# Relative-position steps on other images and stores of queries and keys inside the image loop of an attention kernel

## Chip, cores and metric

The kernel runs on one NeuronCore of a Trainium2 chip. The metric is the device time of one execution in microseconds. The core has TensorE (PE, matrix products), VectorE (DVE), ScalarE (ACT), GpSimd (POOL) and SyncE (SP), which here only issues DMAs. Each engine works through its own program in order and waits on semaphores that others raise.

## The reference

Four layers with group norm before each: a GRU scan (l0), attention with relative positions (l1), a mixture of experts (l2), and again attention (l3). The change touches both attention layers, which run the same code. There are 16 images of 14 x 14 tokens, 12 heads of 16 channels:

```python
attn = jnp.einsum('bqd,bkd->bqk', q * scale, k)
rel_h = jnp.einsum('bhwc,hkc->bhwk', qr, Rh)
rel_w = jnp.einsum('bhwc,wkc->bhwk', qr, Rw)
bias = rel_h[..., :, None] + rel_w[..., None, :]
attn = attn + bias.reshape(B * nh, N, N)
attn = jax.nn.softmax(attn, axis=-1)
out = jnp.einsum('bqk,bkd->bqd', attn, v)
```

For each query, `rel_h` gives 14 numbers for the key's row and `rel_w` 14 for its column. The kernel appends them to the query vector, and 28 selecting zeros and ones to the key vector, so that one product gives logits with bias.

## The kernel before

All is in `attention_layer` (L746). Heads are taken in three quads of four. For each quad, `item` computes queries and keys for all images and writes them, as a rounded part and a rest, into a tile in SBUF (`qk_a` or `qk_b`). They go through DRAM, since the main loop wants them in another layout: `store_qk` (L908) stores a quad's half in five DMAs (one of 784 KB, four of 392 KB), `load` (L922) brings a pair of heads back in four quarters of three pieces each.

The relative numbers take 14 steps for a quad, `rel` on each engine: steps 0 to 6 of them are **row steps** (key row) and 7 to 13 **column steps** (key column). In a step, TensorE issues six products (L1118 to L1120) into one PSUM bank, ScalarE copies the rounded part out (L1262), VectorE subtracts for the rest (L1332). The row steps' tile is stored by `store_rel` (L916) as two DMAs of 686 KB, likewise the column steps' tile. For quads 1 and 2 both tiles have one place in SBUF (`rel_tiles`), so ScalarE waits in front of the first column step until the row tile has landed (L1259).

Quad 0's relative steps stand ahead of the main loop. The **main loop** has 96 image steps (6 pairs of heads x 16 images), here counted from 0. Quad 1's 14 relative steps are put into images 0 to 31 and quad 2's into 32 to 63, at the places in `REL_STEPS` (L751); the text calls 32 images a group: images 0 to 31 are the first group, 32 to 63 the second. In step i the engines do, in this order:

- TensorE (L1198): logits by query of image i (L1133, two banks that need the maximum of i-1 taken), the relative step if there is one, the values products of image i-4 (L1171, L1172; they need VectorE's copies of i-5), the logits by key of i-1 (L1147, L1154; the latter adds the maxima).
- ScalarE (L1291): two exponentials of image i-2 (L1300, L1303), sometimes a copy of values (L1285), the relative step.
- VectorE (L1370): the maximum of image i (L1375), at i % 4 of 2 or 3 a subtraction for the values (L1365), two copies of the products of i-4 (L1340, and L1343 into a ring of three slots of sums), the relative step (L1332), at i % 8 = 1 a reciprocal of the sums (L1347).
- GpSimd (L1061): the rest of the exponentials, a subtraction of 98 x 784 (L1065).
- SyncE, `main_step` (L965): loads of the next pair, a store of quad 2's queries and keys if one is due (L972), `store_rel` in the step behind the last row or column step (L974), a load of the residual (L977), stores of sums at even steps, loads of sums and stores of their reciprocals every eight steps.

The load of a pair's first piece waits for its quad's ten stores (L930), the load of the relative piece for the quad's four relative stores (L932). SyncE's queue is one queue: a wait in it holds all that follows.

Of the kernel before, what the change touches and what calls it, by code (L numbers as in the profile page):

```python
# [745 lines left out]
def attention_layer(nc, tag, ins, x_in, y_out, qk_dram, rel_dram, sums_dram, rec_dram, given=None, kept=None, extra=(), taken=None, ahead=None, x_here=None, x_stored=None):  # L746
# [1 line left out]
    IMAGES = PAIRS * B  # L748
    LAG = 4
    REL = 14  # L750
    REL_STEPS = (1, 2, 3, 4, 5, 6, 7, 11, 12, 13, 14, 15, 16, 17)  # L751
    S_BANK, R_BANK, T_BANK, O_BANK = 0, 2, 3, 7
    REL0_BANK, V_BANK = 4, 6
    EARLY_V = 16
# [3 lines left out]
    with Scope(nc, tag) as s:  # L758
# [71 lines left out]
        def qk_of(quad):  # L830
            return (qk_a, qk_b, qk_a)[quad]
# [26 lines left out]

        rel_of_step = {2 * B * quad + at: REL * (quad + 1) + j for quad in range(QUADS - 1) for j, at in enumerate(REL_STEPS)}

# [15 lines left out]
        with nc.Block() as block:  # L876
            @block.sync
            def _(sp):
# [29 lines left out]
                def store_qk(quad, half, terms=range(5)):  # L908
                    sp.wait_ge(item_low, NT * quad + 4 * half + 4)
                    cols = slice(half * N // 2, (half + 1) * N // 2)  # L910
                    for n in terms:
                        rows, term, part = ((slice(0, 128), 0, 0), (slice(0, 64), 1, 1), (slice(64, 128), 1, 0),
                                            (slice(0, 64), 2, 0), (slice(64, 128), 2, 1))[n]
                        sp.dma_start(qk_dram[quad, rows, term, cols].bitcast(f32), qk_of(quad)[rows, part, cols].bitcast(f32)).then_inc(qk_stored[quad], 16)

                def store_rel(quad, which):  # L916
                    sp.wait_ge(rel_low, REL * quad + 7 * which + 7)
                    for part in range(2):
                        sp.dma_start(rel_dram[quad, :, 2 * part + which, :].bitcast(f32),
                                     rel_tile(REL * quad + 7 * which)[64 * part:64 * part + 56, :].bitcast(f32)).then_inc(rel_stored, 16)  # L920

                def load(p, part, piece):  # L922
                    quad, at = divmod(p, 2)
                    cols = slice(part * EACH * T, (part + 1) * EACH * T)
                    if piece == 0:
                        if p == 0:
                            sp.wait_ge(filled, 2)
                        else:
                            sp.wait_ge(t_summed, B * (p - 1) + EACH * (part + 1))
                        sp.wait_ge(qk_stored[quad], 160)  # L930
                    if piece == (0 if p == 0 else 2):
                        sp.wait_ge(rel_stored, 64 * (quad + 1))  # L932
                    if p == 0 and piece == 2:
                        sp.wait_ge(q_padded, 1)
                    qk = qk_dram[quad].rearrange("(a g h r) c n -> a g r c h n", a=2, g=2, h=2)[:, at].rearrange("a r c h n -> a (r c) h n")
                    rel = rel_dram[quad].rearrange("(g h r) c n -> g r c h n", g=2, h=2)[at].rearrange("r c h n -> (r c) h n")
                    dst, row, src = ((q, Q_ROWS, qk[0]), (k, Q_ROWS, qk[1]), (q, REL_ROWS, rel))[piece]
                    rows = src.shape[0]
                    sp.dma_start(dst[row:row + rows, :, cols].bitcast(f32), src[:, :, cols].bitcast(f32)).then_inc(quarter_in[part], 16)

                def store_sums(g):
                    p, b = divmod(g, B)
                    sp.wait_ge(sums_kept, g + 1)
                    slot, col = g // 2 % SLOTS, (b - 1) % (B // 2) * T
                    sp.dma_start(sums_dram[p, b // (B // 2), :, col:col + TB], ring[:, slot, :]).then_inc(sums_free[slot], 16)

                def load_sums(h):
                    for slot in range(SLOTS):
                        sp.wait_ge(sums_free[slot], 16 * ((B // 4 * (h + 1) - slot + SLOTS - 1) // SLOTS))
                    if h:  # L950
                        sp.wait_ge(rec_low, h)
                    sp.dma_start(sums[:, :], sums_dram[h // 2, h % 2].rearrange("h (c n) -> (h c) n", n=32)).then_inc(sums_in, 16)

                def store_reciprocals(h):
                    p, half = divmod(h, 2)
                    sp.wait_ge(rec_low, h + 1)
                    sp.dma_start(rec_dram[half, :, 2 * p:2 * p + 2, :].rearrange("a h (c n) -> (h c) a n", n=32).bitcast(f32),
                                 rec_parts[:, :, :].bitcast(f32)).then_inc(rec_stored, 16)
# [6 lines left out]
                def main_step(i):  # L965
                    p, b = divmod(i, B)
                    part, piece = divmod(b - EACH - 1, EACH)
                    if i < IMAGES and p + 1 < PAIRS and part >= 0 and piece < LOADS:
                        load(p + 1, part, piece)
                    if i < IMAGES and p > 0 and part < 0 and piece < LOADS:  # L970
                        load(p, part + PARTS, piece)
                    if i % 5 == 3 and i < 50:  # L972
                        store_qk(2, i // 25, [i // 5 % 5])
                    if i - 1 in rel_of_step and rel_of_step[i - 1] % 7 == 6:  # L974
                        quad, j = divmod(rel_of_step[i - 1], REL)
                        store_rel(quad, j // 7)
                    n = (i - 2 * B - REL_STEPS[-1] - 2) // 4  # L977
                    if i == 2 * B + REL_STEPS[-1] + 2 + 4 * n and 0 <= n < NT:
                        if n == 0:
                            sp.wait_ge(rel_summed, QUADS * REL)  # L980
                            sp.wait_ge(qk_stored[2], 160)
                        cols = slice(n * TB, (n + 1) * TB)
                        sp.dma_start(xy[:CP, :, cols], x_in[:, :, cols]).then_inc(x_in_again, 16)
                    g = i - LAG - 1
                    if g >= 0 and g % 2 == 1:
                        store_sums(g)
                    if i >= 14 and i % 8 == 6:
                        load_sums((i - 14) // 8)
                    if i >= 21 and i % 8 == 5:
                        store_reciprocals((i - 21) // 8)  # L990
# [7 lines left out]
                for part in range(PARTS):  # L998
                    for piece in range(LOADS):
                        load(0, part, piece)  # L1000
                for half in range(2):
                    store_qk(1, half)
                for i in range(IMAGES + LAG + 1):
                    main_step(i)
                store_reciprocals(2 * PAIRS - 2)
# [1255 lines left out]
def build(nc, ins, out):  # L2261
    scratch = {n: nc.dram_tensor(n, sh, f32r if n in ("qk", "rel", "rec") else f32, kind="Internal").ap() for n, sh in
               (("x1", [CP, CB, N]), ("x2", [C, N]), ("x3", [C, N]), ("qk", [QUADS, 128, 3, N]), ("rel", [QUADS, 56, 4, N]), ("sums", [PAIRS, 2, 2, N // 2]), ("rec", [2, 2, HEADS, N // 2]),
                ("rows", [N, 256]), ("picked", [2 * N + BLOCKS * LANES, C]))}

    def halves(x):
        return x.rearrange("(k p) n -> p k n", k=CB)

    with Scope(nc, "to") as s:
        moments, x_stored = s.sb("moments", [128, 2, B, 2]), s.sem("x_stored")  # L2270
        first = Ahead(nc, "l1")
        x_sb = first.place(AT_Q, CB, N)[:CP]
        averages = [first.place(AT_AVERAGES, CP)[:CP], first.place(AT_AVERAGES + CP, CB, 2, 128)[:CP]]
        ahead = dict(xh=first.place(0, CB, N, dt=f32r), weights=first.weights()[:4], avg=dict(avg=first.place(AT_AVG, CP)[:CP]))
        gru_layer(nc, ins, ins["x"], scratch["x1"], x_sb, x_stored, moments, ahead)
        attention_layer(nc, "l1", ins, scratch["x1"], halves(scratch["x2"]), scratch["qk"], scratch["rel"], scratch["sums"], scratch["rec"],
                        kept=moments, extra=((averages[0], ins["group_avg"]), (averages[1], ins["avg_out128"])), taken=moments[:CP], ahead=ahead, x_here=x_sb, x_stored=x_stored)
        third = Ahead(nc, "l3")
        later = dict(weights=third.weights(), avg=dict(avg=third.place(AT_AVG, 2, 2, 128), avg_out=third.place(AT_AVG + 512, 2, CB, CP)))
        experts_layer(nc, ins, scratch["x2"], scratch["x3"], scratch, moments, later, averages)  # L2280
        attention_layer(nc, "l3", ins, halves(scratch["x3"]), out, scratch["qk"], scratch["rel"], scratch["sums"], scratch["rec"], given=moments, ahead=later)
# [132 lines left out]
```

## Time and profile before

| | us |
|---|---|
| median of 3 runs | 1782.19 (1781.6 to 1787.44) |
| profiled execution | 1781.53 |
| its span on the core | 1779.3 |
| PE / DVE / ACT / POOL busy | 1477.8 / 1251.0 / 899.5 / 800.3 |

The span is the stretch from the first to the last instruction that the profiler shows; 2.2 us of the execution lie around it. Busy time is a sum over stages. The main loop of l1 runs from 643 to about 900 us, that of l3 from 1472 to about 1731 us. L numbers are lines of the kernel before; "SPq" is SyncE's queue.

### The profile page before, as it was taken

The page shows a single profiled execution, that of the slowest core. Times are in us where ns is not written, and L with a number is a line of the kernel's source. Part 1 is how long each engine was busy: PE and PEld are TensorE (multiplying, and loading weights), DVE is VectorE, ACT ScalarE, POOL GpSimd, SP SyncE. Part 2 cuts the span into 40 slices and gives each one's busy share as a digit, 9 for nine tenths or more (in the row PEclk, how much of TensorE's full clock was granted, in tenths as well). Part 3 has the DMA queues.
Part 4 walks back from the last instruction along what each step waited for, and adds up shares of the span by engine and source line. Part 5 has one row for each costly group of instructions (what it writes and reads, how often), then busy time and mean ns, then how long its engine had stood idle before and what let it go on. Part 6 is the DMA issues. An engine that isn't in the chain of part 4 may idle for free. (4 is left out here: it accounts for less than half of the span.)

```text
span 1779.3 us, 50706 instructions
## 1 busy us (share of the span) xinstructions
PE 1477.8 (83%) x19315; PEld 1308.6 (74%) x19315; DVE 1251.0 (70%) x4156; ACT 899.5 (51%) x1894; POOL 800.3 (45%) x888
## 2 busy tenths in 40 slices
PE   4868888888876886989976989899998697888977
PEld 4757777777765685878965667688884587787976
DVE  7877877877878656878856694544446646887874
ACT  3633333333345665767833433555553555666862
POOL 2812222222226054758952210556651415676974
PEclk9955555555558898999987589999995689999998
DMA  3000000000002585658415304333225458666812
GB/s 88 1 21 4 4 4 4 4 4 4 4 4 84 152 241 150 154 138 172 96 37 160 126 14 148 114 96 93 87 78 154 145 149 266 162 140 145 162 31 58
DMA packets 71882, 164.52 MB, mean 92 GB/s; under 512 B 17842, under 2 KB 43066, under 8 KB 69148
## 3 DMA queue, kind: packets, MB, share of 16 engines
q1 hardware_dynamic: 66268, 148.44, 31.6%
q0 software_dynamic: 5376, 12.85, 2.4%
q8 instruction: 156, 2.56, 0.6%
q14 instruction: 82, 0.67, 0.1%
HBM read 93.84 MB, written 67.42 MB: 91 GB/s over the span
## 5 line engine op out<-in xcount | busy, mean ns | idle before, releaser
L1065 POOL TENSOR_TENSOR l_arena<-l_arena,l_arena 98x784 fp32r<-98x784 f32 x192 | 360.5, 1881 | 136.5 <-ACT l_arena L1303 132.0
L514 PE MATMUL gru_ps_r<-gru_hp,gru_wp 128*128 128x16 f16 x3920 | 199.7, 176 | 68.3 <-DVE gru_hp L489 68.3
L514 PEld LDWEIGHTS gru_ps_r<-gru_hp,gru_wp 128*128 128x128 f16 x3920 | 150.4, 105 | 88.7 <-DVE gru_hp L489 88.7
L1300 ACT ACTIVATE l_arena<-l_ps 98x784 fp32r<-98x784 f32 x192 | 158.6, 826 | 103.7 <-PE l_ps L1154 101.7
L1375 DVE TENSOR_REDUCE l_mt<-l_ps 98x4 fp32r<-98x784 f32 x192 | 186.8, 973 | 27.4 <-PE l_ps L1133 22.9
L514 PE MATMUL gru_ps_n<-gru_hp,gru_wp 128*128 128x16 f16 x3920 | 191.2, 174 | 0.0
L567 POOL TENSOR_TENSOR gru_kept<-gru_keep,l0s_state 128x32 f32<-128x32 f32 x196 | 49.3, 252 | 305.9 <-ACT gru_keep L582 305.9
L1171 PE MATMUL l_ps<-l_arena,l_arena 128*66 128x196 f32 x768 | 162.7, 264 | 22.3 <-DVE l_arena L1343 20.7
L580 ACT ACTIVATE gru_reset<-gru_ps_r,gru_unscale 128x32 f32<-128x32 f32 x196 | 56.5, 288 | 216.9 <-PE gru_ps_r L514 216.9
L1172 PE MATMUL l_ps<-l_arena,l_arena 128*66 128x196 f32 x768 | 158.9, 259 | 0.0
L1303 ACT ACTIVATE l_arena<-l_ps 98x784 f32<-98x784 f32 x192 | 157.2, 819 | 0.0
L514 PEld LDWEIGHTS gru_ps_n<-gru_hp,gru_wp 128*128 128x128 f16 x3920 | 150.0, 104 | 0.0
L1171 PEld LDWEIGHTS l_ps<-l_arena,l_arena 128*66 128x66 f32 x768 | 108.9, 142 | 37.8 <-issue 20.1
L1172 PEld LDWEIGHTS l_ps<-l_arena,l_arena 128*66 128x66 f32 x768 | 109.5, 143 | 1.1
L1133 PE MATMUL l_ps<-l_arena,l_arena 128*98 128x196 f32 x768 | 104.0, 258 | 6.7 <-DVE l_mt L1375 4.0
L1154 PE MATMUL l_ps<-l_unit,l_mt 98*98 98x196 f32 x768 | 105.3, 260 | 0.0
L1147 PE MATMUL l_ps<-l_arena,l_arena 128*98 128x196 f32 x768 | 103.9, 259 | 0.0
L1340 DVE COPY l_arena<-l_ps 64x196 f32<-64x196 f32 x192 | 67.6, 352 | 50.1 <-PE l_ps L1172 47.2
L1118 PE MATMUL l_ps<-l_arena,l_arena 128*56 128x224 f32 x168 | 58.9, 351 | 48.7 <-DVE l_arena L1332 45.8
L1262 ACT ACTIVATE l_arena<-l_ps 56x448 fp32r<-56x448 f32 x84 | 63.1, 751 | 68.0 <-PE l_ps L1120 46.5
L2215 DVE TENSOR_TENSOR l_arena<-mx_ps,l_arena 128x512 fp32r<-128x512 f32 x56 | 38.7, 692 | 83.1 <-ACT l_arena L2023 83.1
L1332 DVE TENSOR_TENSOR l_arena<-l_ps,l_arena 56x448 fp32r<-56x448 f32 x84 | 65.0, 775 | 41.0 <-ACT l_arena L1262 39.2
(386 smaller groups left out, 4512.9 us busy)
## 6 DMA issues: line engine op xcount, KB each, us to landing
l_arena<-qk SPq DMA_DIRECT2D x96, 294.0 KB
qk<-l_arena SPq DMA_DIRECT2D x48, 392.0 KB, 6.0
rel<-l_arena SPq DMA_DIRECT2D x24, 686.0 KB
l_arena<-rel SPq DMA_DIRECT2D x48, 343.0 KB
qk<-l_arena SPq DMA_DIRECT2D x12, 784.0 KB, 10.5
l_arena<-in_experts_dram SPq DMA_DIRECT2D x8, 1152.0 KB, 7.5
l_arena<-x SPq DMA_DIRECT2D x24, 294.0 KB, 5.5
l_arena<-x SPq DMA_DIRECT2D x24, 196.0 KB, 4.2
```

The lines of the kernel that those rows point to most:

```text
L514: last = pe.matmul(out[:, b, B * m:B * m + B], wp[:, wi, g, m, :], hp[:, b, part, B * k:B * k + B], start=False, stop=True, skip_group_che ...
L1065: pool.tensor_tensor(pl[g % LOWS][:TH, :, :], p32[:TH, g % 2, :, :], ph[:TH, g % 4, :, :].bitcast(f32), ALU.subtract).then_inc(pl_ready, 1)
L1133: last = pe.matmul(ps[:TH, S_BANK + head, half * T:half * T + T], q[:, head, queries], k[:, head, keys], start=True, stop=True)
L1147: pe.matmul(bank[:, half * T:half * T + T], k[:, head, keys], q[:, head, queries], start=half == 0, stop=False, skip_group_check=True)
L1154: last = pe.matmul(bank[:, :, half * TH:(half + 1) * TH], mt[:TH, g % 2, n:n + 1].to_broadcast([TH, TH]), both, start=False, stop=half == ...
L1171: pe.matmul(out, values, ph[:, g % 4, head, cols], start=head == 0 and keys == 0, stop=False)
L1172: last = pe.matmul(out, values, pl[g % LOWS][:, head, cols], start=False, stop=head == 1 and keys == 1)
L1300: act.activation(ph[:TH, g % 4, :, :], banks, ACT.Exp).then_inc(p_high, 1)
L1303: act.activation(p32[:TH, g % 2, :, :], banks, ACT.Exp).then_inc(p_ready, 1)
L1332: dve.tensor_tensor(rel_out(r, 64), rel_sums(r), rel_out(r, 0).bitcast(f32), ALU.subtract).then_inc(rel_low, 1)
L1340: dve.tensor_copy(o_quad[p // 2][row:row + 64, b * T:(b + 1) * T], ps[:64, O_BANK, :T]).then_inc(o_kept, 1)
L1375: dve.tensor_reduce(mt[:TH, i % 2, :], ps[:TH, S_BANK:S_BANK + 2, :TB].rearrange("p c (h k) -> p c h k", h=2), AXIS.X, ALU.max, negate=Tru ...
```

## The change

```diff
-    REL_STEPS = (1, 2, 3, 4, 5, 6, 7, 11, 12, 13, 14, 15, 16, 17)
+    REL_STEPS = (0, 1, 2, 3, 4, 5, 6, 10, 12, 14, 16, 18, 20, 21)
...
-                    if i % 5 == 3 and i < 50:
-                        store_qk(2, i // 25, [i // 5 % 5])
+                    if 9 <= i < 19:
+                        store_qk(1, (i - 9) // 5, [(i - 9) % 5])
+                    if 23 <= i < 53 and i % 3 == 2:
+                        store_qk(2, (i - 23) // 15, [(i - 23) // 3 % 5])
...
-                for half in range(2):
-                    store_qk(1, half)
                 for i in range(IMAGES + LAG + 1):
                     main_step(i)
```

The row steps move from images 1 to 7 to images 0 to 6 of each group, the column steps from 11 to 17 to 10, 12, 14, 16, 18, 20 and 21. The ten stores of quad 1, all issued ahead of the loop, are issued one a step at steps 9 to 18. Quad 2's ten stores go from steps 3, 8, ..., 48 to 23, 26, ..., 50. What hangs on `REL_STEPS` moves with it: the stores of relative tiles from steps 8 and 18 of a group to 7 and 22, and the residual's eight loads (L977) from 51, 55, ... to 55, 59, .... No instruction is added or removed.

## Rows read from the trace of the kernel before

**Rows 1.** The page's head: the span.

```profile
span 1779.3 us, 50706 instructions
```

**Rows 2.** Windows: us, PE, PEld, DVE, ACT, POOL busy, clock, DMA share, GB/s.

```profile
643.04:738.82 95.78, 76.23 (x685) 70.23 (x686) 68.76 (x118) 60.29 (x88) 59.19 (x38) 0.93 0.72 200
738.82:830.65 91.83, 80.04 (x725) 73.79 (x726) 74.91 (x131) 62.49 (x95) 61.87 (x41) 0.96 0.63 145
830.65:895.83 65.18, 62.31 (x637) 59.30 (x637) 58.22 (x116) 52.40 (x81) 61.56 (x41) 1.00 0.50 100
...
1472.57:1564.31 91.74, 76.05 (x685) 69.73 (x686) 68.43 (x117) 60.31 (x88) 59.08 (x38) 0.96 0.76 211
1564.31:1657.04 92.73, 80.94 (x725) 75.07 (x726) 74.91 (x131) 62.46 (x95) 61.93 (x41) 0.94 0.63 144
```

**Rows 3.** Timeline (start, us, engine, line), ScalarE: the first column step of each group.

```profile
680.62 0.92 ACT L1262 ACTIVATE l_arena<-l_ps 56x448 fp32r<-56x448 f32 x1 [9.18 <-DMA rel<-l_arena]
...
772.59 0.92 ACT L1262 ACTIVATE l_arena<-l_ps 56x448 fp32r<-56x448 f32 x1 [2.12 <-DMA rel<-l_arena]
...
1507.61 0.93 ACT L1262 ACTIVATE l_arena<-l_ps 56x448 fp32r<-56x448 f32 x1 [6.63 <-DMA rel<-l_arena]
...
1598.93 0.93 ACT L1262 ACTIVATE l_arena<-l_ps 56x448 fp32r<-56x448 f32 x1 [2.03 <-DMA rel<-l_arena]
```

**Rows 4.** Timeline, VectorE: last row steps of three groups, and a wait at step 10.

```profile
663.96 0.62 DVE L1332 TENSOR_TENSOR l_arena<-l_ps,l_arena 56x448 fp32r<-56x448 f32 x1
...
763.00 0.62 DVE L1332 TENSOR_TENSOR l_arena<-l_ps,l_arena 56x448 fp32r<-56x448 f32 x1
...
1493.50 0.62 DVE L1332 TENSOR_TENSOR l_arena<-l_ps,l_arena 56x448 fp32r<-56x448 f32 x1
...
1502.02 0.36 DVE L1343 COPY l_arena<-l_ps 2x196 f32<-2x196 f32 x1 [2.62 <-DMA sums<-l_arena]
```

**Rows 5.** Timeline, VectorE: from one column step to the next (steps 15, 16).

```profile
698.29 0.92 DVE L1332 TENSOR_TENSOR l_arena<-l_ps,l_arena 56x448 fp32r<-56x448 f32 x1
699.25 0.98 DVE L1375 TENSOR_REDUCE l_mt<-l_ps 98x4 fp32r<-98x784 f32 x1
701.46 0.35 DVE L1340 COPY l_arena<-l_ps 64x196 f32<-64x196 f32 x1 [1.23 <-PE l_ps L1172]
701.84 0.36 DVE L1343 COPY l_arena<-l_ps 2x196 f32<-2x196 f32 x1
702.23 0.92 DVE L1332 TENSOR_TENSOR l_arena<-l_ps,l_arena 56x448 fp32r<-56x448 f32 x1
```

**Rows 6.** Timeline, TensorE: the same column step.

```profile
699.27 0.39 PE L1118 MATMUL l_ps<-l_arena,l_arena 128*56 128x224 f32 x1 [0.69 <-DVE l_arena L1332]
...
700.51 0.28 PE L1171 MATMUL l_ps<-l_arena,l_arena 128*66 128x196 f32 x1
...
701.25 0.52 PE L1147 MATMUL l_ps<-l_arena,l_arena 128*98 128x196 f32 x4
701.61 0.53 PE L1154 MATMUL l_ps<-l_unit,l_mt 98*98 98x196 f32 x4
```

**Rows 7.** Timeline, VectorE and GpSimd: two pairs of operations that meet.

```profile
691.92 1.76 DVE L1365 TENSOR_TENSOR l_arena<-l_arena,l_arena 98x128 fp32r<-98x128 f32 x1
...
691.67 1.86 POOL L1065 TENSOR_TENSOR l_arena<-l_arena,l_arena 98x784 fp32r<-98x784 f32 x1 [1.50 <-ACT l_arena L1303]
...
758.31 0.28 DVE L1365 TENSOR_TENSOR l_arena<-l_arena,l_arena 98x128 fp32r<-98x128 f32 x1
...
758.35 1.97 POOL L1065 TENSOR_TENSOR l_arena<-l_arena,l_arena 98x784 fp32r<-98x784 f32 x1 [1.23 <-ACT l_arena L1303]
```

**Rows 8.** TensorE at step 19: timeline, then a window (columns of Rows 2).

```profile
710.58 0.40 PE L1171 MATMUL l_ps<-l_arena,l_arena 128*66 128x196 f32 x1 [1.58 <-DVE l_arena L1343]
...
711.00:713.00 2.00, 2.00 (x14) 2.00 (x14) 1.34 (x4) 0.00 (x0) 0.96 (x3) 0.50 0.84 257
```

**Rows 9.** The stores at L914 issued from 636 to 650 us: time to landing.

```profile
DMA to landing us min/median/max: 13.7/16.1/24.7
```

## The prediction

> **What bounds the kernel now.** I read the profile page first for the span [rows 1], then the windows of the main loop of both attention layers [rows 2]. There, 32 images ("a group") without relative steps take 65.18 us, 2.04 us an image, and TensorE is busy for 62.31 of them. A group that carries 14 relative steps takes 91.83 us (layer l1, second group), and TensorE is busy for 80.04 only. The first groups carry the same work and take 95.78 and 91.74 us. So each group with relative steps costs 27 to 31 us more than a plain one, and TensorE's own part in that is about half. The rest is waits, and the change moves just the steps that cause them. Two kinds stand out.
>
> First, the column tile takes the place of the row tile in SBUF (`rel_tiles`), so ScalarE may write the first column step only when the row tile has landed in DRAM (L1260). It waited 9.18 us for that in l1's first group and 6.63 in l3's, but 2.12 and 2.03 in the second groups [rows 3]. From the end of VectorE's last row step to ScalarE's first column step are 16.0 and 13.5 us in first groups, and 9.0 in a second one [rows 3, 4]. The transfer is the same. What differs is the queue: in first groups the ten stores of quad 1's queries and keys stand ahead of it, and they took 13.7 to 24.7 us from issue to landing [rows 9].
>
> Second, a chain through three engines in consecutive column steps. VectorE's rows show it from one step to the next [rows 5]: the step's subtraction (0.92 us, L1332), the maximum (0.97, L1375), 1.23 us idle until TensorE's values product is done, two copies (0.38 each with their pitch), the next subtraction. That is 3.94 us, from 698.29 to 702.23. TensorE starts its relative products 0.06 us after the subtraction ends, issues them for 1.24 us, and only then the values products, 0.74 us [rows 6], because its program has the relative step in front of them. So in this stretch an image lasts 3.93 us instead of 2.04, and neither engine is full.
>
> **The change part by part.**
>
> *Column wait.* The stores of quad 1 leave the place ahead of the loop and go out one a step at steps 9 to 18. The row store goes out at SyncE's step 7 (before: 8), the first column step is step 10 (before: 11), so three plain images lie between, as before. Ahead of it in the queue is then what a second group has: three loads. So I give the first groups the second groups' wait. By ScalarE's idle time that is 9.18 - 2.12 = 7.1 us in l1. In l3 it is 6.63 - 2.12 = 4.5, with VectorE's wait of 2.62 us for a slot of the sums [rows 4] in the shadow of the same column wait, and not added. Sum: -11.6 us. The second groups keep their 2.1 us, as their row store still has its 9 us to go. Bounds: -15 if the queue is even emptier (each group's wait halved), 0 if the first groups still wait as long.
>
> *Columns apart.* Laid out in program order, a column step and the plain image behind it give this loop: logits by query 0.37 (four products of that size lie 0.36 apart, [rows 6]), relative products 1.24, values products 0.74 and 0.21 until VectorE sees them, two copies 0.77, subtraction 0.95, the maximum of the next image 1.03, after which TensorE may overwrite the logits bank for the image after next. That is 5.31 us for the pair. Before, one consecutive column step and one plain image elsewhere took 3.93 + 2.04 = 5.97. Each column step that gets a plain neighbour saves 0.66 us. Before, one of the seven had one (step 17); after, six do, as only 20 and 21 adjoin. Five times 0.66 is 3.3 us a group, and -13.2 us for four groups. TensorE's own issue time in the pair is 2 x 1.84 + 1.24 = 4.9, so it cannot go below 5 us for a pair; the lower bound is -20.
>
> *What takes most of that back.* VectorE's subtraction for the values (L1365), twice in four images, shows a duration of 0.28 us when it starts just before GpSimd's subtraction, and 1.76 when it starts 0.25 us into one: it ends 0.15 us after GpSimd's does [rows 7]. The Trainium skill, page "SBUF — State Buffer", section "Who interferes with whom", says that a VectorE instruction with two SBUF inputs contends with a GpSimd one that reads SBUF, and that the second to start is blocked for the whole instruction of the first; the two rows agree. In consecutive column steps the wait lies mostly inside the 1.23 us for TensorE and costs 0.35 us at step 14; at step 18 it is open, and TensorE then idles 1.58 us [rows 8] where 0.6 would be usual: 1.0. Together 1.4 a group. In the pair loop VectorE asks 1.54 us after TensorE starts the logits by query, and GpSimd's operation, freed by ScalarE's second exponential, starts at about 1.45: VectorE comes just too late, and the copies start at 3.35 instead of 2.56, 0.8 us late; in the plain half it asks 0.4 us into the next one. Laying steps 10 to 23 out so, four of the eight L1365 land openly: steps 11 (0.8), 14 (1.0), 18 (1.0) and 22 (1.4), 4.2 us. That is 2.8 more than before in each group, +11.2 us. Bounds: 0 if VectorE wins the close race of 0.1 us, as in the row steps; +20 if all land openly.
>
> *Rows on 0 to 6.* In a first group the eight images from 643.04 to 664.61 hold seven row steps (the latter number is the end of the row-step subtraction, [rows 4]). Step 0 has no values products and TensorE waits there for the first maximum anyway, so a row step costs about 0.4 us there and frees 1.2 at step 7: -0.8 in each first group, -1.6. In second groups step 32 is like any other: 0.
>
> *Sums behind the column store.* SyncE's step 22 now issues the column store (two of 686 KB), then a store of sums, then a load of sums, and step 23 waits until the column store has landed. VectorE's reciprocal of step 25 needs that load; by the layout it comes 9.2 us after the last column subtraction, and the column store alone takes about 9 [rows 3, 4]. I take a stall of 1 us a group, +4, with bounds 0 and 3 a group (the one such wait shown is 2.62, [rows 4]). Behind SyncE's wait stand one store and one load, and a store of sums whose slot VectorE needs four images later: free.
>
> *Ten stores inside the loop.* Each is one issue on SyncE, of 784 KB (one in five) or 392 KB, 470 on average; with the 230 KB of loads that an image has, the queue carries 700 KB in an image of 2.7 us, some 265 GB/s. The first group as it was ran at 200 GB/s with the DMA engines busy for 0.72 of the time [rows 2], which makes 278 when full, so it just fits; cost 0, as quad 2's key loads need it only from step 21. Quad 2's stores every third image instead of every fifth, and the residual's load four images later (step 55), have over 30 images before their readers: 0.
>
> *Clock.* After the 1.58 us idle at step 19 the granted clock was 0.50 for about 3 us [rows 8], some 1.5 us lost. The layout has one idle stretch of 2 us at step 23 in its place, so 0 net; bounds -4 and +7 over four groups.
>
> Sum: -11.6 - 13.2 + 11.2 - 1.6 + 4 = -11.2 us. The profiled execution took 1781.53 (span 1779.3); 1781.53 - 11.2 = 1770.3. The median of the three runs lies 0.7 higher, so the forecast is 1771.0.
>
> **Rivals.**
>
> A, the port is not hit. VectorE wins the race by GpSimd's start, as it does at 758.31 [rows 7]; then the 11.2 us of waits don't come: 1760. For it: the margin is 0.1 us. Against: ScalarE's two exponentials and the maximum both hang on TensorE's order, and every plain stretch would have to fall the same way.
>
> B, the column wait stays. The change to the stores doesn't do what it seems to, because the row store is slowed by what is issued behind and before it (loads of three pieces, stores of steps 9 and 10, which share its 16 engines). Then the 11.6 us stay: 1782.6, no change. For it: the second groups take 9 us for 1.4 MB without those stores. Against: second groups have loads ahead of it and behind it too, and it lands in 9 us all the same.
>
> C, the clock. The pair loop has idle stretches of 0.4 to 0.8 us in each pair and the 2 us at step 23; if each group gets one more stretch at 0.50, 1.7 us each, the time is 1771 + 6.8 = 1778. The row of 0.69 us idle in every column step [rows 6], at full clock, speaks against it.
>
> D, slower. The queue is full from step 9 on, and what matters is the sums. If stores and loads need more than the 2.7 us of an image, the backlog grows by perhaps 1 us an image, and from about 10 us on VectorE's copies wait for slots (four to five images of slack), as they did once for 2.62 us. Over the ten stores that is 8 us in each of two first groups, and 3 us at step 25 in four: 1771 + 16 + 8 = 1795, slower than before. It decides from a rate of the queue below about 260 GB/s in steps 9 to 18.
>
> **How the numbers follow.** Forecast 0.54, A 0.16, B 0.10, C 0.10, D 0.10. The range reaches from A's 1760 to 1780, past C; it leaves out B and D, 0.20. A measurement of this kernel can tell about 0.3%, 5.3 us, from no change. Faster by more than that (below 1776.8): nearly all of the forecast and A and a third of C, 0.72. Within it: B, the rest of C and some of the forecast, 0.18. Slower: D, 0.10.
>
> **What would show it.** ScalarE's waits for the row tile should be about 2 us in all four groups. VectorE's maxima of steps 12 to 20 should alternate between about 2.0 to 2.8 and 2.7 to 4.6 us. L1365 should show durations near 1.7 us at four steps a group. A wait of the reciprocal for sums should be at step 25 and 57, about 1 us. The forecast is wrong if the row store takes over 11 us to land, if L1365 runs in 0.28 us throughout (then A), or if VectorE's copies wait for DMA (then D).

## The result, and the profile after

The changed kernel takes 1765.3 us (median of 4 runs, 1762.6 to 1768.3) against 1784.8 us of the kernel before (4 runs). The ratio is 0.9889, with a 95% interval of 0.9856 to 0.9923: 19.6 us faster at the medians. The forecast was 11.2 us faster, in a range of 2 to 22. Run again beside the experiments, on one chip, the ratio was 0.9909 (0.9886 to 0.9932), some 16 us.

The windows of the changed kernel's main loops answer to [rows 2]; the columns are the same, and the first four are the groups with relative steps (first and second of l1, first and second of l3), the fifth the plain one.

```profile
642.94:727.67 84.73, 73.84 (x686) 66.99 (x685) 71.63 (x117) 60.19 (x88) 59.14 (x38) 1.00 0.75 204
727.67:818.64 90.97, 79.91 (x725) 73.51 (x724) 77.76 (x131) 62.30 (x95) 61.77 (x41) 0.96 0.67 160
1466.56:1554.11 87.55, 76.36 (x686) 69.75 (x685) 71.00 (x118) 60.18 (x88) 59.14 (x38) 0.96 0.74 200
1554.11:1643.35 89.24, 77.64 (x727) 70.84 (x726) 77.83 (x130) 62.65 (x95) 62.12 (x41) 1.00 0.67 161
818.64:883.80 65.16, 62.23 (x636) 59.25 (x637) 58.06 (x116) 52.40 (x81) 61.60 (x41) 1.00 0.55 111
```

The four groups took 372.1 us before and 352.5 now, 19.6 us less (352.1 in the changed kernel's second profile). The plain images are as they were. The reader may miss something: the span fell by 13.7 us only, from 1779.3 to 1765.6. The other 6 us lie between the two attention loops, from the last maximum of l1 to the first of l3. The engines' work there is the same; of the change, only the stores of l3's quad 1 reach into the last 5 us of it. This stretch took 578.8 us before and 584.8 and 586.3 in the two profiles of the changed kernel, and 577.2 to 590.4 in the twelve profiles of this study. It goes with TensorE's clock: the same products kept TensorE busy for 501.5 us before (mean granted clock 0.84) and for 508.8 and 508.7 after (0.83). Why the clock differs there is open, and with one profile for most kernels it can't be said whether it belongs to a kernel or to an execution. So the loops are compared group by group, and a kernel's whole time is read from its runs.

ScalarE's first column steps, with their waits, answer to [rows 3] (timeline):

```profile
670.61 0.96 ACT L1262 ACTIVATE l_arena<-l_ps 56x448 fp32r<-56x448 f32 x1 [1.93 <-DMA rel<-l_arena]
...
760.25 0.96 ACT L1262 ACTIVATE l_arena<-l_ps 56x448 fp32r<-56x448 f32 x1 [1.75 <-DMA rel<-l_arena]
...
1494.66 0.96 ACT L1262 ACTIVATE l_arena<-l_ps 56x448 fp32r<-56x448 f32 x1 [2.33 <-DMA rel<-l_arena]
...
1585.97 0.96 ACT L1262 ACTIVATE l_arena<-l_ps 56x448 fp32r<-56x448 f32 x1 [1.96 <-DMA rel<-l_arena]
```

All four are at about 2 us, as forecast; the 9.18 and 6.63 are gone. In l1's first group SyncE issues the row store at 661.85 and ScalarE goes on 8.8 us later.

The starts of VectorE's maxima (L1375) mark the images. The table gives their distances in us, so that a group's time can be seen stage by stage. "Column wait" is the stage in which ScalarE waits for the row tile; "no low" (without L1365) and the other names are the experiments below. Most rows show one group of a kernel.

| kernel, group | images 0-8 | 8-10 | 10-12 (column wait) | 12-24 | 24-32 | all |
|---|---|---|---|---|---|---|
| before, l1 first | 21.6 | 3.8 | 14.1 | 39.7 | 16.6 | 95.8 |
| before, l1 second | 24.8 | 3.8 | 7.0 | 39.7 | 16.5 | 91.8 |
| before, l3 first | 21.6 | 3.8 | 11.6 | 38.2 | 16.6 | 91.7 |
| before, l3 second | 25.8 | 3.8 | 7.0 | 39.6 | 16.6 | 92.7 |
| changed, l1 first | 20.7 | 3.9 | 8.2 | 35.5 | 16.5 | 84.7 |
| changed, l1 second | 25.6 | 4.1 | 7.9 | 35.9 | 17.4 | 91.0 |
| changed, l3 first | 20.7 | 3.9 | 8.6 | 37.9 | 16.4 | 87.5 |
| changed, l3 second | 24.7 | 4.1 | 8.2 | 35.5 | 16.8 | 89.2 |
| e1 (steps only), l1 first | 20.7 | 3.9 | 15.5 | 37.9 | 16.4 | 94.5 |
| e2 (stores only), l1 first | 22.6 | 3.8 | 6.8 | 39.7 | 16.5 | 89.4 |
| e2 (stores only), l3 first | 21.6 | 3.8 | 7.3 | 39.6 | 16.6 | 88.8 |
| e5 (before, no low), l1 second | 23.5 | 3.8 | 6.9 | 35.9 | 15.8 | 85.9 |
| e5 (before, no low), l3 second | 23.5 | 3.8 | 7.0 | 36.2 | 16.4 | 86.9 |
| e6 (changed, no low), l1 second | 23.3 | 4.0 | 6.9 | 33.9 | 16.6 | 84.7 |
| e6 (changed, no low), l3 second | 23.3 | 4.0 | 6.9 | 33.3 | 17.0 | 84.5 |
| e3 (columns chosen), l1 second | 24.7 | 4.1 | 5.6 | 35.4 | 21.9 | 91.7 |
| e7 (reciprocals later), l1 second | 23.4 | 4.0 | 6.0 | 35.5 | 16.6 | 85.5 |
| e4 (low on GpSimd), l1 first | 20.7 | 3.9 | 6.8 | 33.4 | 18.5 | 83.2 |
| e8 (e4 and e7), l1 first | 20.7 | 3.9 | 6.8 | 33.3 | 18.0 | 82.8 |
| e9 (e8, columns chosen), l1 first | 20.7 | 3.9 | 5.7 | 34.7 | 16.2 | 81.2 |

### The profile page after: what moved, and what is told of

The parts are those of the page before. It is cut to its first block and busy times, and to the rows that moved or that the text cites. A ratio compares the mean times of both kernels' runs of the same rounds, so it can differ in the third digit from the quotient of the medians.

```text
span 1765.6 us, 50706 instructions
## 1 busy us (share of the span) xinstructions
PE 1478.4 (84%) x19315; PEld 1304.8 (74%) x19315; DVE 1260.3 (71%) x4156; ACT 898.6 (51%) x1894; POOL 802.0 (45%) x888
## 5 line engine op out<-in xcount | busy, mean ns | idle before, releaser
L1375 DVE TENSOR_REDUCE l_mt<-l_ps 98x4 fp32r<-98x784 f32 x192 | 187.0, 974 | 24.0 <-PE l_ps L1133 19.2
L1171 PE MATMUL l_ps<-l_arena,l_arena 128*66 128x196 f32 x768 | 159.1, 260 | 26.6 <-DVE l_arena L1343 25.4
L1172 PE MATMUL l_ps<-l_arena,l_arena 128*66 128x196 f32 x768 | 155.3, 255 | 0.0
L1171 PEld LDWEIGHTS l_ps<-l_arena,l_arena 128*66 128x66 f32 x768 | 106.6, 139 | 43.2 <-issue 32.8
L1133 PE MATMUL l_ps<-l_arena,l_arena 128*98 128x196 f32 x768 | 104.9, 259 | 16.0 <-DVE l_mt L1375 13.2
L1172 PEld LDWEIGHTS l_ps<-l_arena,l_arena 128*66 128x66 f32 x768 | 107.2, 140 | 0.8
L1133 PEld LDWEIGHTS l_ps<-l_arena,l_arena 128*98 128x98 f32 x768 | 86.1, 167 | 21.7 <-issue 12.2
```

Of the source, the lines that this page charges most:

```text
L1133: last = pe.matmul(ps[:TH, S_BANK + head, half * T:half * T + T], q[:, head, queries], k[:, head, keys], start=True, stop=True)
L1171: pe.matmul(out, values, ph[:, g % 4, head, cols], start=head == 0 and keys == 0, stop=False)
L1172: last = pe.matmul(out, values, pl[g % LOWS][:, head, cols], start=False, stop=head == 1 and keys == 1)
L1375: dve.tensor_reduce(mt[:TH, i % 2, :], ps[:TH, S_BANK:S_BANK + 2, :TB].rearrange("p c (h k) -> p c h k", h=2), AXIS.X, ALU.max, negate=Tru ...
```

## The experiments

### e1 and e2: each half of the change alone

e1 has the new `REL_STEPS` and leaves all stores of queries and keys where they were; e2 is the reverse.

```diff
# e1, against the kernel before
-    REL_STEPS = (1, 2, 3, 4, 5, 6, 7, 11, 12, 13, 14, 15, 16, 17)
+    REL_STEPS = (0, 1, 2, 3, 4, 5, 6, 10, 12, 14, 16, 18, 20, 21)
# e2, against the changed kernel
-    REL_STEPS = (0, 1, 2, 3, 4, 5, 6, 10, 12, 14, 16, 18, 20, 21)
+    REL_STEPS = (1, 2, 3, 4, 5, 6, 7, 11, 12, 13, 14, 15, 16, 17)
```

> Only the relative steps move (rows to 0 to 6, columns to 10, 12, 14, 16, 18, 20, 21); quad 1's ten stores stay ahead of the loop. Theory 1 (the moved stores bring most of the gain; the spacing of the columns is eaten up by VectorE's subtraction L1365 waiting for GpSimd's): in both first groups ScalarE's first column step lands at the same distance from the loop's start as before, 37.6 us in l1 and 35.0 in l3, since the row tile still stands behind the same queue; its wait grows to about 11 and 9 us because it asks two us earlier. First groups 95 and 92 us, second groups about 91, total within 3 us of before (ratio 0.998 to 1.002). Theory 2 (spacing is the gain, at 3.3 us a group): 8 to 13 us faster, ratio 0.993 to 0.995.

> Only the stores move (quad 1's to steps 9 to 18, quad 2's to 23 to 50); the relative steps stay at 1 to 7 and 11 to 17. Theory 1: ScalarE's wait for the row tile falls to about 2 us in the first groups, which last some 87.5 us; second groups as before, 91 to 92; total 13 us less than before (ratio 0.991 to 0.994), two thirds of what the whole change brings. Theory 2: the stores bring less than 5 us, ratio above 0.997.

> The changed kernel itself, beside the others on one chip. Theory 1: ratio 0.988 to 0.992, groups of 85, 91, 88 and 89 us as in its first profile. What it gains over the kernel with the stores alone moved (some 5 us) is the first row step in the pipeline's fill and the later column steps.

Measured: e1 0.9993 (0.9973 to 1.0012), e2 0.9934 (0.9912 to 0.9957), the whole change 0.9909 (0.9886 to 0.9932). The first fence is e1's timeline, ScalarE's first column steps of the first groups; the second is e2's.

```profile
676.97 0.92 ACT L1262 ACTIVATE l_arena<-l_ps 56x448 fp32r<-56x448 f32 x1 [9.27 <-DMA rel<-l_arena]
...
1513.38 0.92 ACT L1262 ACTIVATE l_arena<-l_ps 56x448 fp32r<-56x448 f32 x1 [7.06 <-DMA rel<-l_arena]
```

```profile
673.86 0.92 ACT L1262 ACTIVATE l_arena<-l_ps 56x448 fp32r<-56x448 f32 x1 [1.93 <-DMA rel<-l_arena]
...
1503.87 0.92 ACT L1262 ACTIVATE l_arena<-l_ps 56x448 fp32r<-56x448 f32 x1 [2.34 <-DMA rel<-l_arena]
```

The wait goes with the stores alone. The stage 10-12 falls from 14.1 to 6.8 us in l1 and from 11.6 to 7.3 in l3: 11.6 us, the term of the sum. e2 moves quad 2's stores as well as quad 1's; that the second groups of before waited 2.1 us with quad 2's stores at 33 and 38 in front speaks for quad 1's, but no run moves them alone. In e1 the wait stays. In l1 the first column step came 35.1 us after the first maximum and in l3 32.8, where 37.6 and 35.0 were expected, so the waits are 9.27 and 7.06 us instead of the 11 and 9 expected; why the tile landed over 2 us earlier is open. By the groups of these profiles e1 gives 5.9 us, e2 9.2 (a stretch at half clock in images 0 to 8 of l1, which the kernel before lacks, costs it 1), the whole change 19.6. That the halves help each other, since time saved ahead of a late transfer is waited away again, fits these groups; the runs' ratios (0.9993, 0.9934 and 0.9909) are too close to each other to show it. In the runs' times e1 gives nothing that could be told from zero.

The groups of the changed kernel's second profile took 86.2, 89.4, 87.1 and 89.5 us (85, 91, 88 and 89 in the first), and its ratio lies in the 0.988 to 0.992 expected.

### e3 and e7: the columns where the port is free

The rule that L1365 and GpSimd's subtraction block each other, laid out with the durations of the trace of before, gives another placing that should be better. e3 has it; e7 adds one line. ("Port" here and in the expectations stands for this meeting of the two operations.)

```diff
# e3, against the changed kernel
-    REL_STEPS = (0, 1, 2, 3, 4, 5, 6, 10, 12, 14, 16, 18, 20, 21)
+    REL_STEPS = (0, 1, 2, 3, 4, 5, 6, 11, 13, 14, 15, 17, 18, 19)
# e7, against e3 (VectorE)
-                    if i >= 17 and i % 8 == 1:
-                        reciprocals((i - 17) // 8)
+                    if i >= 19 and i % 8 == 3:
+                        reciprocals((i - 19) // 8)
```

> As the changed kernel, but the column steps at 11, 13, 14, 15, 17, 18 and 19, found by laying the durations of the trace of before out in program order with the rule that L1365 and GpSimd's subtraction block each other. Theory 1 (the port decides what a placing of the columns is worth): the L1365 of these steps mostly meet no running GpSimd operation, so that at most one or two a group last over 1 us instead of four to six; groups of 82 and 87 us, total 8 to 12 us less than the changed kernel (ratio to before 0.981 to 0.985). Theory 2 (only the free neighbours count): this one has fewer of them (three against six) and is 2 us a group slower than the changed kernel, ratio 0.993.

e3 measured 0.9893 (0.987 to 0.9916): 3 us less than the changed kernel, not 8 to 12. Its stages 10-24 take 41 us instead of 44, as they should, but images 24 to 31 take up to 21.9 us instead of 16.5. VectorE's timeline shows why, at steps 25 and 57 of both layers:

```profile
712.66 0.35 DVE L1347 RECIPROCAL l_sums<-l_sums 98x32 f32<-98x32 f32 x1 [0.61 <-DMA l_sums<-sums]
...
803.73 0.35 DVE L1347 RECIPROCAL l_sums<-l_sums 98x32 f32<-98x32 f32 x1 [3.29 <-DMA l_sums<-sums]
...
1532.53 0.35 DVE L1347 RECIPROCAL l_sums<-l_sums 98x32 f32<-98x32 f32 x1 [1.35 <-DMA l_sums<-sums]
...
1622.20 0.35 DVE L1347 RECIPROCAL l_sums<-l_sums 98x32 f32<-98x32 f32 x1 [2.67 <-DMA l_sums<-sums]
```

It is a wait for sums whose load stands behind the column store, which the prediction had put into the changed kernel.

> As the run with the columns at 11, 13, 14, 15, 17, 18, 19, but VectorE's reciprocals two images later (i % 8 of 3 instead of 1). There, the reciprocal of step 25 waited 0.6 to 3.3 us for its sums, which stand in the queue behind the column store, and images 24 to 31 took 18.5 and 21.9 us instead of 16.5. Theory 1 (this is the whole of the loss): no such wait, images 24 to 31 back at 16.5 us, groups of 82 and 86 us, total 12 to 15 us less than the changed kernel (ratio to before 0.981 to 0.984). Theory 2 (the full queue delays something else): groups stay at 84 and 91 us, ratio 0.989.

e7 measured 0.9829 (0.9804 to 0.9855), 1750.5 us. Images 24 to 31 are back at 16.6 us and the groups take 82.5 and 85.5 us in both layers. Theory 1 holds with its numbers. (About 1.3 us in each second group have another place: images 32 to 40 take 23.4 us instead of 24.7, and the L1365 of step 34, 1.85 us in all kernels with the early reciprocals, is short.) The count of long L1365 expected for e3 is wrong: e7 has four of over 1 us in steps 10 to 23 of a group, at 14, 15, 18 and 19, and the kernel before had three, at 14, 15 and 18. What the placing changes is what they cost. From image 10 to 24, e7 takes 41.3 us and e9 below, which has the same steps without them, 40.4: 0.9 us. With the changed kernel's steps the same comparison is 43.7 against e8's 40.2: 3.5 us.

### e5 and e6: both kernels without L1365

```diff
# e5, e6: VectorE; TensorE then waits for ScalarE's part (vh_ready) instead
-                    if 8 <= i < IMAGES and i % 4 in (2, 3):
-                        lower_values(n, i % 4 - 2)
```

> The kernel before without the loop's 92 low-part subtractions of the values (L1365; from the third round of values on the low parts keep what stood there, so the output leaves that part of the computation out). Theory 1 (L1365 and GpSimd's subtraction block each other): beside the 0.28 us that each needs, the waits go: 20 us less than before, ratio 0.987 to 0.991. Theory 2 (the long durations cost nothing since VectorE waits anyway): under 8 us, ratio above 0.995.

> The changed kernel without L1365 in the loop, as the run beside it. Theory 1: the waits behind GpSimd eat a good part of what the spacing of the columns gives; without them the same change is worth 25 to 28 us instead of 16 to 19, so this one is 43 to 48 us faster than the kernel before (ratio 0.973 to 0.977). Theory 2 (the port has nothing to do with the change): the difference to the run beside it is the 16 to 19 us of the change itself, ratio 0.979 or more.

(There are 88 of them in the two loops, not 92.) Measured: e5 0.9853 (0.9834 to 0.9871), 26 us less than before, more than theory 1 said; e6 0.977 (0.975 to 0.9791), 41 us less. So the 88 operations cost some 26 us in either kernel, and the change is worth 15 us without them and 16 with them, which is the second theory's number. But e6 pays something that e5, the kernel before and the changed kernel don't: VectorE's reciprocals wait 1.4 us for sums in l1's two groups and 2.1 in l3's, and more in the plain images behind (images 64 to 95 take 61.4 and 61.8 us, e5's 60.3 and 60.1). And what e5 takes away is the operation with its own 0.28 us, not the meeting alone: 5.7 of its 26 us come from the plain images, where no L1365 lasts over 0.6 us.

The stages say it more closely. From image 10 to 24 of second groups, the kernel before takes 46.7 and 46.5 us and e5 42.8 and 43.2: L1365 costs 3.9 and 3.4. In the first groups, taken from image 12 so that the column wait stays out, it costs 3.4 and 2.0. That is 12.7 us in four groups. The changed kernel takes 43.7, 43.9, 46.5 and 43.7 us from 10 to 24 and e6 40.1, 40.8, 41.4 and 40.2: 15.2 us in four groups, and 15.0 by the changed kernel's second profile. So L1365 eats some 2.5 us more of the changed kernel than of the kernel before. The spacing by itself, e5 against e6 from image 12 to 24, is worth 3.0, 2.0, 2.4 and 2.8 us in the four groups, 10.2 in all, where the prediction had 3.3 each. In e6 a plain image and a column image last 1.7 + 3.7 = 5.4 us, where the prediction laid out 5.31.

### e4, e8 and e9: GpSimd does the subtraction

e4 moves L1365's work behind GpSimd's own operation; e8 does so only in the two groups with relative steps, and has e7's later reciprocals; e9 is e8 with e3's columns. The call is shortened in the cut below.

```diff
# e8, against the changed kernel (GpSimd, behind L1065)
+                    n = g // 4 + 1
+                    if g >= 6 and n < 16 and g % 4 in (2, 3):
+                        head = g % 4 - 2
+                        pool.wait_ge(vh_ready, 2 * n + head + 1)
+                        pool.tensor_tensor(value_parts(n, head, 1), values_of(n, head), ..., ALU.subtract)
# VectorE
-                    if 8 <= i < IMAGES and i % 4 in (2, 3):
+                    if 4 * B <= i < IMAGES and i % 4 in (2, 3):
```

> The changed kernel with L1365's subtraction done by GpSimd, behind its own, instead of by VectorE. Theory 1: no two operations meet any more; if GpSimd needs 0.4 us for it, 5 us a layer are saved, 10 in all against the changed kernel (ratio to before 0.984 to 0.987); the plain images are the risk, since GpSimd is busy for 61.6 of 65.2 us there and gets 6 us more. Theory 2: GpSimd becomes the bound of plain images, 2.1 us an image instead of 2.04, and the loop is no faster.

e4 measured 0.9825 (0.9799 to 0.9851), 1748.4 us. Both theories have a part in it: groups fall to 82 to 85 us (theory 1 had 10 us in all; the groups alone give 18), and the plain images, where GpSimd is nearly full, get slower: 31 of them take 64.7 and 65.2 us instead of 63.1 (1.7 of the latter is a wait of a reciprocal for sums). GpSimd is busy there for 33.1 of 33.4 us, where it was 30.9 of 32.5 in the changed kernel. It needs 0.44 us for the operation (groups by line, count and mean in ns):

```profile
L1065 POOL TENSOR_TENSOR l_arena<-l_arena,l_arena 98x784 fp32r<-98x784 f32 x96 | 179.1, 1876 | 37.5 <-ACT l_arena L1308 37.4
L1071 POOL TENSOR_TENSOR l_arena<-l_arena,l_arena 98x128 fp32r<-98x128 f32 x44 | 19.3, 439 | 0.0
```

> The changed kernel with two additions: GpSimd does L1365's subtraction in the two groups that carry relative steps, VectorE in the plain images behind them; and VectorE's reciprocals come two images later (i % 8 of 3). From the runs so far: groups of 81 us (20.7 + 3.9 + 6.8 + 33.4 + 16) and 83 us (23.3 for the first eight images), plain images as in the kernel before (63.1 us for 31), no wait for sums in images 24 to 31. Over four groups 24 us less than the changed kernel, ratio to before 0.976 to 0.979. If the wait for sums was not what made images 24 to 31 long there (17 to 18.5 us), the groups stay at 83 and 85 us and the ratio at 0.981.

> As the run beside it, with the column steps at 11, 13, 14, 15, 17, 18, 19. If placing mattered only because of operations that meet (theory 1), it is now worth nothing, since none meet in these groups: the same within 3 us (ratio between the two 0.998 to 1.002), with consecutive column steps of 3.9 us and no wait for the row tile. If free neighbours count by themselves (5.3 us for a column step and a plain image against 5.9), the spaced one is 2 us a group faster, less the 1.8 us that it waits for the row tile.

e8 measured 0.9806 (0.9776 to 0.9836), which misses its 0.976 to 0.979. VectorE's waits in e8's two groups of l1 show where it stayed:

```profile
DVE l_arena L1345 <- PE l_ps L1177: 20.6, 24, 1.2
DVE l_arena L1337 <- ACT l_arena L1267: 6.2, 6, 1.7
DVE l_mt L1380 <- PE l_ps L1138: 3.6, 11, 0.4
DVE l_arena L1348 <- DMA sums<-l_arena: 3.2, 3, 1.9
```

(L1348 is L1343 of the kernel before, and L1352 in e4 its L1347.) In e4 the reciprocal waited 4.0 us in all for sums in the same stretch; in e8 it doesn't, and now the copy into the ring waits 3.2 us for a free slot. So moving one reader of a small transfer two images back let the next one wait in its place, and the second reading given for e8 was nearer: the groups stay at 83 to 84 us.

A second cost was not foreseen: the handover. In l3 of e8, VectorE's first subtraction, at step 66, comes while GpSimd works off its own without a pause, and its 0.28 us become 2.67:

```profile
1623.68 2.67 DVE L1370 TENSOR_TENSOR l_arena<-l_arena,l_arena 98x128 fp32r<-98x128 f32 x1
```

The image lasts 4.4 us, and the 31 plain images 65.3 us instead of 63.1. In e9 both layers have such an operation (2.66 and 2.03 us long) and plain images of 66.6 and 65.2 us; a half-clock stretch behind it has a part in the former.

e9 measured 0.9784 (0.9755 to 0.9813), 1742.4 us, the fastest kernel of this study that leaves nothing out: 39 us less than before, 24 less than the changed kernel at the medians. Its median is 5 us under e8's, more than the 3 expected, but the two intervals overlap, so they can't be told apart. The stages can: from image 10 to 24 the spaced columns of e8 take 40.2 us in l1's first group and e9's 40.4, the 0.2 us that the second reading gave (1.3 us lost in 12-24, 1.1 gained in 10-12, where the wait for the row tile is gone). e9's last column step is 19 instead of 21, so the column store goes out two images earlier, and no wait for sums is left in images 24 to 31 (16.2 us, where e8 has 16.1 to 18.0).

## Why the prediction was right, and where its sum was not

The changed kernel is faster for the reasons given, and its time lies in the range. The forecast of 11.2 us was still 8 short of the 19.6 that the groups gained (5 short of the second comparison's 16), and most errors of the sum lie on one side. That the time fell inside is owed to the width of the range, and not to the sum.

**Column wait, -11.6 us: right in mechanism and size.** e2 shows it alone, 7.3 and 4.3 us in the stage against 7.1 and 4.5. Rival B (the wait stays) is excluded by the four waits of 2 us.

**Columns apart, -13.2 us: right mechanism, somewhat large.** e5 against e6 gives 2.0 to 3.0 us a group, 10.2 in all, instead of 3.3 a group.

**What takes it back, +11.2 us: wrong in size, and this is the term of the sum that failed.** The meeting of L1365 and GpSimd's operation is as described. VectorE's timeline of the changed kernel, steps 11 and 14, against GpSimd's (x2: two of its operations in one line):

```profile
672.57 0.97 DVE L1375 TENSOR_REDUCE l_mt<-l_ps 98x4 fp32r<-98x784 f32 x1
673.46 1.56 DVE L1365 TENSOR_TENSOR l_arena<-l_arena,l_arena 98x128 fp32r<-98x128 f32 x1
...
680.20 0.97 DVE L1375 TENSOR_REDUCE l_mt<-l_ps 98x4 fp32r<-98x784 f32 x1
681.09 1.89 DVE L1365 TENSOR_TENSOR l_arena<-l_arena,l_arena 98x128 fp32r<-98x128 f32 x1
682.90 0.35 DVE L1340 COPY l_arena<-l_ps 64x196 f32<-64x196 f32 x1
```

```profile
673.01 3.75 POOL L1065 TENSOR_TENSOR l_arena<-l_arena,l_arena 98x784 fp32r<-98x784 f32 x2 [2.33 <-ACT l_arena L1303]
679.12 3.71 POOL L1065 TENSOR_TENSOR l_arena<-l_arena,l_arena 98x784 fp32r<-98x784 f32 x2 [2.36 <-ACT l_arena L1303]
```

The long ones are at steps 11, 14, 18 and 22, the four that the prediction named (1.56, 1.89, 1.68 and 1.69 us), in three of four groups; in l3's first group step 15 has the long one instead of 14. The images that start at these steps last 3.1, 4.4, 4.2 and 3.4 us. So rival A is out. Image by image against e6, in l1's first group, they cost 0.5, 0.7, 0.8 and 1.6 us where the prediction had 0.8, 1.0, 1.0 and 1.4: 3.6 instead of 4.2. The larger error was in what the same thing cost before. I took 1.4 us a group for it; the kernel before against e5 shows up to 3.9. In l1's second group this is 0.3 at step 14 (0.35 said), 1.4 at step 18 (1.0 said), 1.4 in image 19 and 0.8 spread over the others. The L1365 of step 15, 1.4 us long, which the prediction left out, cost nothing. Image 19's part is the half clock (a granted clock of 0.50, the lower of TensorE's two levels) behind the idle stretch [rows 8], which I had booked as a term of its own with a net of 0. It belonged to this one: image 19 lasts 3.6 us in three groups and 2.2 in l3's first, which had no such stretch there, and without L1365 (e5) 2.1 in all four. With 12.7 us before and 15.2 after in four groups, the term is about +2.5, not +11.2.

**Clock, 0 net: about 2 us too high.** The kernel before has a half-clock stretch at step 19 in three of four groups, some 1.5 us each; the changed kernel has one behind the idle stretch of step 23 in two of four (l1's second and l3's first), where images 23 and 24 together take 5.5 us instead of 4.1. Both are in the stages counted above and below. In l1's first group it idles 1.87 us there, more than the 1.58 before, and the windows behind it are at full clock (timeline, then windows, TensorE's clock being the third number from the end):

```profile
709.16 0.28 PE L1171 MATMUL l_ps<-l_arena,l_arena 128*66 128x196 f32 x1 [1.87 <-DVE l_arena L1343]
```

```profile
708.00:709.00 1.00, 0.00 (x0) 0.00 (x0) 0.94 (x3) 0.01 (x1) 1.00 (x2) 1.00 0.78 176
709.00:710.00 1.00, 0.84 (x10) 0.87 (x10) 0.97 (x3) 0.00 (x0) 0.95 (x1) 1.00 0.73 176
710.00:711.00 1.00, 1.00 (x13) 0.99 (x11) 0.93 (x4) 0.16 (x1) 0.00 (x0) 1.00 0.72 253
```

The same kernel's second profile has the same stretch in the same group, 1.86 us, and half clock behind it:

```profile
708.26 0.28 PE L1171 MATMUL l_ps<-l_arena,l_arena 128*66 128x196 f32 x1 [1.86 <-DVE l_arena L1343]
```

```profile
710.00:711.00 1.00, 1.00 (x9) 1.00 (x8) 0.34 (x2) 0.92 (x2) 0.00 (x0) 0.50 0.89 226
```

So what sets the one or the other is not the length of the stretch alone, and the 2 us are chance, not gain to count on. What it is stays open. Rival C, a stretch more in each group, did not occur: two of four groups have one behind step 23 in each profile.

**Rows on 0 to 6, -1.6 us: right.** The first eight images take 20.7 us in both first groups instead of 21.6: -1.8. (664.61, which the prediction calls the end of the row-step subtraction, is the start of image 8's maximum; the subtraction ends at 664.58 [rows 4].)

**Sums behind the column store, +4 us: nothing came of it here.** The last column subtraction of l1's first group ends at 705.63, and the reciprocal runs at 714.85 without a wait, 9.2 us later, the distance that the prediction gave. The stall of 1 us that it took for this distance was not there:

```profile
704.67 0.96 DVE L1332 TENSOR_TENSOR l_arena<-l_ps,l_arena 56x448 fp32r<-56x448 f32 x1
...
714.85 0.33 DVE L1347 RECIPROCAL l_sums<-l_sums 98x32 f32<-98x32 f32 x1
```

In e4 VectorE is faster there and waits until 10.2 us behind the same point:

```profile
701.28 0.96 DVE L1337 TENSOR_TENSOR l_arena<-l_ps,l_arena 56x448 fp32r<-56x448 f32 x1
...
712.47 0.35 DVE L1352 RECIPROCAL l_sums<-l_sums 98x32 f32<-98x32 f32 x1 [2.65 <-DMA l_sums<-sums]
```

So the mechanism is real, and the changed kernel escapes it; e6, without L1365, has it too (waits of up to 1.2 us). That it is the changed kernel's long L1365 of step 22 which holds VectorE up for long enough fits both, but when the sums landed there was not read.

Rival D rested on the same queue and on a rate below about 260 GB/s in steps 9 to 18. The changed kernel moved 275 GB/s there in l1 (the line below) and 264 in l3, with the DMA engines busy for 0.88 and 0.84 of the time. (The 700 KB of the prediction in 2.7 us are 259 GB/s, not 265.)

```profile
665.67:696.27 30.60, 26.61 (x240) 23.63 (x239) 27.45 (x42) 22.12 (x32) 19.71 (x12) 1.00 0.88 275
```

The largest waits for DMA inside its groups are the four of about 2 us for the row tile, so D did not occur. Waits for ring slots of up to 1.9 us came in e8, where VectorE is faster.

With the measured sizes: -11.6 for the wait, -10.2 for the columns, +2.5 for L1365 (the half clock of step 19 in it), -1.8 for the rows, 0 for the sums. Two small things come on top: images 8 to 10 take 0.1 to 0.3 us longer in each group, +0.7, and images 24 to 31 +0.8, which is the half clock behind step 23 of l1's second group. This makes -19.6, what the groups gave. By the runs, the whole change is worth 16 to 20 us.

## What to carry to other kernels

Before a late transfer is shortened or work is moved ahead of it, look at what stands in front of it in its queue: here ten large stores that nobody needed for twenty images held up one that was needed after three, and moving only the work gained nothing that the runs could show. When a stall is costed on both sides of a change, its aftermath (here the half clock behind an idle stretch) must be booked with the stall on both sides, or it is counted once too little. A placing that is better by the engines' order can expose a small transfer queued behind a large one; here it helped to put its reader two images later (e7), and the next reader then waited in one of two cases (e8, but not e9).

## What the runs showed of the hardware beyond this

Idle stretches of TensorE of 1.5 to 1.9 us were followed by a granted clock of 0.50 in some places and not in others: in the kernel before 1.58 us and 0.50 [rows 8], but in l3's first group 1.57 us and no half clock; in the changed kernel, at the same step of the same group, 1.87 us and 1.00 in one execution and 1.86 us and 0.50 in the other.

A subtraction of 98 x 128 costs VectorE 0.28 us alone, 1.4 to 1.9 us when it meets GpSimd's, and 2.7 us when GpSimd does its own one behind the other; GpSimd takes 0.44 us for it. Leaving the 88 of them out saved 26 us of 1781. Where they stand matters as much as how long they last: four long ones in a group cost 3.5 us with the changed kernel's column steps and 0.9 us with e7's.
